# Attention scores with the halves of Q stacked on the contraction axis: two 256-column matmuls for a batch entry instead of three, the low part applied by ScalarE and the mask by GpSimd

## What is computed

```python
x = x + einsum('bct,bcd->bdt', x, w0[idx])          # 32 batch entries of 128 x 1024
q, k, v = heads(x @ Wq.T), heads(x @ Wk.T), heads(x @ Wv.T)   # 16 heads of 64
scores = einsum('bhqd,bhkd->bhqk', q * min(cond, 4), k) / sqrt(64)
attn = softmax(where(causal, scores, lowest))         # 128 x 128 per head
x = x + merge(einsum('bhqk,bhkd->bhqd', attn, v)) @ Wo.T
```

## Time and profile before

| what | value |
|---|---|
| median of 3 runs | 1558.01 us (1557.51 to 1558.75) |
| the profiled execution | 1558.96 us |
| its span, first to last instruction | 1557.5 us |
| PE busy | 1547.1 us (99%), 7459 matmuls |
| DVE, ACT, POOL busy | 1034.9, 840.9, 866.6 us (66, 54, 56%) |
| mean granted clock | 0.998 |

### The profile page before, as it was taken

One profiled execution on the slowest core, in us unless ns is written; L12 is line 12 of the kernel. 1 busy time (PEld: TensorE's weight loads), 2 busy tenths in 40 slices (PEclk: granted clock), 3 DMA queues, 4 the chain that ended last, 5 costly groups with the idle time before them and its releaser, 6 DMA issues.

```text
span 1557.5 us, 23477 instructions
## 1 busy us (share of the span) xinstructions
PE 1547.1 (99%) x7459; PEld 1302.0 (84%) x7459; DVE 1034.9 (66%) x1891; ACT 840.9 (54%) x2286; POOL 866.6 (56%) x752
## 2 busy tenths in 40 slices
PE   9999999999999999999999999999999989999999
PEld 7888888888888888888888888888888878888887
DVE  5867677664477777777767777777777644555553
ACT  6666566652466666666655666666666622222220
POOL 1555665662365566557655576575577545555552
PEclk9999999999999999999999999999999999999999
DMA  9968988866766677767677466677665696444442
GB/s 324 335 230 278 319 307 296 294 254 231 273 190 198 201 214 209 205 184 191 182 240 229 147 179 202 194 200 200 180 188 157 237 366 226 162 168 163 162 167 83
DMA packets 192300, 341.46 MB, mean 219 GB/s; under 512 B 23986, under 2 KB 116402, under 8 KB 185010
## 3 DMA queue, kind: packets, MB, share of 16 engines
q1 hardware_dynamic: 191026, 331.59, 66.2%
q10 hardware_dynamic: 1152, 8.39, 1.4%
HBM read 184.70 MB, written 134.22 MB: 205 GB/s over the span
## 4 chain that ended last, share of the span: by engine, by line
PE 95%; DVE 2%; DMA 1%; SPq 1%; POOL 0%; issue 0%; ACT 0%; DVEq 0%; POOLq 0%
PE p_PJ L768 22%; PE p_PJ L769 22%; PE p_PJ L770 22%; PE p_SC L770 6%; PE p_SC L769 6%; PE p_SC L768 6%; PE p_PV L873 4%; PE p_LP L768 1%; PE p_PV L768 1%; PE p_PV L770 1%; PE p_PV L769 1%; PE p_LP L770 1%; PE p_LP L769 1%; DVE t_WSL L1285 1%; DVE t_TS L1281 1%; DMA out<-t_xr 0%
## 5 line engine op out<-in xcount | busy, mean ns | idle before, releaser
L769 PE MATMUL p_PJ<-t_XL,t_WH 128*128 128x512 f32 x1008 | 394.2, 391 | 0.0
L768 PE MATMUL p_PJ<-t_XH,t_WH 128*128 128x512 f32 x1008 | 394.2, 391 | 0.0
L770 PE MATMUL p_PJ<-t_XH,t_WL 128*128 128x512 f32 x1008 | 392.1, 389 | 0.0
L1118 ACT ACTIVATE t_PP<-t_PP,t_st 128x128 f32<-128x128 f32 x512 | 199.5, 391 | 174.9 <-DVE t_st L1314 173.3
L1438 POOL TENSOR_TENSOR t_PP<-t_PP,t_st 128x512 f32<-128x512 f32 x128 | 133.2, 1041 | 205.8 <-DVE t_st L1318 205.8
L770 PEld LDWEIGHTS p_PJ<-t_XH,t_WL 128*128 128x128 f32 x1008 | 189.3, 188 | 40.5
L768 PEld LDWEIGHTS p_PJ<-t_XH,t_WH 128*128 128x128 f32 x1008 | 190.0, 188 | 33.8
L769 PEld LDWEIGHTS p_PJ<-t_XL,t_WH 128*128 128x128 f32 x1008 | 190.0, 188 | 32.3
L1332 DVE TENSOR_REDUCE t_AT<-p_PV 64x256 f32<-64x512 f32 x252 | 171.3, 680 | 24.5 <-ACT t_AC L1136 12.1
L1444 POOL TENSOR_TENSOR t_AT<-t_AT,t_AC 128x256 f32<-128x256 f32 x126 | 117.1, 929 | 126.2 <-DVE t_AT L1332 126.2
L1441 POOL TENSOR_TENSOR t_PS<-t_PT,t_PS 128x512 fp32r<-128x512 f32 x122 | 157.6, 1292 | 0.0
(11 more groups left out here) (259 smaller groups left out, 3597.7 us busy)
## 6 DMA issues: line engine op xcount, KB each, us to landing
t_XH<-xth_scratch SPq DMA_DIRECT2D x56, 512.0 KB, 6.4
t_XL<-xtl_scratch SPq DMA_DIRECT2D x56, 512.0 KB, 6.7
t_PT<-t_TB SPq DMA_DIRECT2D x580, 32.0 KB, 2.3
v_scratch<-t_VR SPq DMA_DIRECT2D x64, 256.0 KB, 4.6
xth_scratch<-t_XH SPq DMA_DIRECT2D x16, 1024.0 KB, 4.5
xtl_scratch<-t_XL SPq DMA_DIRECT2D x16, 1024.0 KB, 6.8
t_VX<-v_scratch SPq DMA_DIRECT2D x32, 512.0 KB, 5.6
at_scratch<-t_AT SPq DMA_DIRECT2D x126, 128.0 KB, 3.4
```

The costliest lines, as they stand in the source:

```text
L768: pe.matmul(bank, lh, rh, start=first, stop=False, skip_group_check=goes_on)
L769: pe.matmul(bank, lh, rl, start=False, stop=False, skip_group_check=goes_on)
L770: return pe.matmul(bank, ll, rh, start=False, stop=last, skip_group_check=goes_on)
L1118: act.activation(PP[:, u, h, :], PP[:, u, h, :], ACT.Exp, bias=st[:, 0, u, h:h + 1], scale=1.0, accum_out=st[:, 1, u, h:h + 1]).then_inc(a ...
```

## The change

Q's high half of one head (64 rows) and its low half (64 rows) are stacked on the 128 rows of the contraction axis in `QM[h]`; `KM[h]` holds K's high half twice in its first 128 columns, and in the other 128, on the high rows only, its low half (the rest zeros). One matmul per head with 256 columns then gives (qh*kh + ql*kh) in the first 128 columns and qh*kl in the other. The two parts have to be added afterwards: ACT writes beta times the second part into `PP`, POOL adds the mask, and DVE adds beta times the first part. The scores of one batch entry now fill a bank of their own, three banks in turn, `SC[0]`, `SC[1]`, `LP`.

```diff
-        KH = sb("KH", [128, GB, 256], f32r)
-        KL = sb("KL", [128, GB, 256], f32r)
-        QH = sb("QH", [128, T], f32r)
-        QL = sb("QL", [128, T], f32r)
+        KM = [sb(f"KM{h}", [128, GB, 256], f32r) for h in range(2)]
+        QM = [sb(f"QM{h}", [128, T], f32r) for h in range(2)]
...
-                late = 2.5 if n else 0
+                late = 5 if n else 0
                 q_ev.put(done + late, n)
                 ql_ev.put(done + late + 1, n)
                 done += 8
                 kh_ev.put(done + 0.25, n)
                 kl_ev.put(done + 1, n)
-                a = done + 5
+                a = done + 7
                 for u in range(GB):
-                    k = u // 2
-                    sc_at.put(a + k, GB * n + u)
-                    mask_at.put(a + 1 + 2 * k, GB * n + u)
-                    exp_at.put(a + (2, 3, 4, 5)[u], GB * n + u)
-                move_at.put(a + 10, n)
+                    sc_at.put(a + (0, 0.5, 1, 4.5)[u], GB * n + u)
+                    low_at.put(a + (0.75, 1.25, 1.75, 5.25)[u], GB * n + u)
+                    add_at.put(a + (1.25, 2, 3, 6)[u], GB * n + u)
+                    mask_at.put(a + (2.5, 3.5, 4.5, 7.25)[u], GB * n + u)
+                    exp_at.put(a + (3.5, 4.5, 5.5, 8.25)[u], GB * n + u)
+                move_at.put(a + 12.5, n)
                 for k in range(2):
                     P = 2 * n + k
-                    recip_at.put(a + 4 + 2 * k, P)
-                    norm_at.put(a + 4.25 + 2 * k, P)
-                    turn_at.put(a + 7.5 + 1.5 * k, P)
+                    recip_at.put(a + (6.25, 9.25)[k], P)
+                    norm_at.put(a + (6.5, 9.5)[k], P)
+                    turn_at.put(a + (9, 12)[k], P)
                     last = n == 4 * NGRP - 1
-                    half_at.put(a + (20 if last else 25.25) + 0.5 * k, P)
-                    ptl_at.put(a + (20.75 if last else 26) + 1.5 * k, P)
-                    v = a + (27.25 + 3.25 * k if last else 29 + 4.5 * k)
+                    half_at.put(a + (22.5 if last else 26) + 0.5 * k, P)
+                    ptl_at.put(a + (23.25 if last else 26.5) + 1.5 * k, P)
+                    v = a + (29.25 + 3.25 * k if last else 29 + 4.5 * k)
                     own = v + (1.75 if n >= 4 * NGRP - 2 else (1.75, 8.5)[k])
...
-            early = t - PAIR
+            early = t - PAIR + (5 if q == 0 else 0)
...
+        def s_bank(U):
+            return (SC[0], SC[1], LP)[U % 3][:].rearrange("p (h l k) -> p h l k", h=2, l=2)
...
+                pe.wait_ge(act_k, 4 * n + 4)
...
-            three(SC[z][:, 256 * (u % 2):256 * (u % 2) + 256], QH[:, cols], QL[:, cols], KH[:, u, :], KL[:, u, :], True, True).then_inc(pe_sc, 1)
+            if U >= 3:
+                pe.wait_ge(dve_s, U - 2)
+            for h in range(2):
+                mm = pe.matmul(s_bank(U)[:, h].rearrange("p l k -> p (l k)"), QM[h][:, cols], KM[h][:, u, :], start=True, stop=True)
+            mm.then_inc(pe_sc, 1)
...
                     for h in range(2):
                         r = slice(64 * h, 64 * h + 64)
-                        act.activation(KH[r, :, 128 * h:128 * h + 128], pj[r], ACT.Copy).then_inc(act_k, 1)
+                        other = slice(64 - 64 * h, 128 - 64 * h)
+                        act.activation(KM[h][r, :, 0:128], pj[r], ACT.Copy).then_inc(act_k, 1)
+                        act.activation(KM[h][other, :, 0:128], pj[r], ACT.Copy).then_inc(act_k, 1)
...
-                    act.activation(QH[:], PJ[bank_of["q", n]][:], ACT.Copy).then_inc(act_q, 1)
+                    for h in range(2):
+                        r = slice(64 * h, 64 * h + 64)
+                        act.activation(QM[h][r], PJ[bank_of["q", n]][r, :], ACT.Copy).then_inc(act_q, 1)
+                for U in low_at(tick):
...
+                    act.wait_ge(pe_sc, U + 1)
...
+                    act.activation(PP[:, u], s_bank(U)[:, :, 1], ACT.Copy, scale=beta[:, bb:bb + 1]).then_inc(act_l, 1)
...
                 for n in ql_ev(tick):
-                    dve.wait_ge(act_q, n + 1)
-                    dve.tensor_tensor(QL[:], PJ[bank_of["q", n]][:], QH[:].bitcast(f32), ALU.subtract).then_inc(dve_q, 1)
+                    for h in range(2):
+                        r, other = slice(64 * h, 64 * h + 64), slice(64 - 64 * h, 128 - 64 * h)
+                        dve.wait_ge(act_q, 2 * n + h + 1)
+                        dve.tensor_tensor(QM[h][other], PJ[bank_of["q", n]][r, :], QM[h][r].bitcast(f32), ALU.subtract).then_inc(dve_q, 1)
                 for U in mask_at(tick):
...
-                    dve.scalar_tensor_tensor(
-                        out=PP[:, u], in0=SC[u // 2][:, 256 * (u % 2):256 * (u % 2) + 256].rearrange("p (h k) -> p h k", h=2), scalar=beta[:, bb:bb + 1],
-                        in1=mask[:].unsqueeze(1).to_broadcast([128, 2, 128]), op0=ALU.mult, op1=ALU.add).then_inc(dve_s, 1)
+                    dve.wait_ge(pool_m, U + 1)
+                    dve.scalar_tensor_tensor(out=PP[:, u], in0=s_bank(U)[:, :, 0], scalar=beta[:, bb:bb + 1],
+                                             in1=PP[:, u], op0=ALU.mult, op1=ALU.add).then_inc(dve_s, 1)
...
+                for U in add_at(tick):
...
+                    pool.wait_ge(act_l, U + 1)
+                    pool.tensor_tensor(PP[:, U % GB], PP[:, U % GB], mask[:].unsqueeze(1).to_broadcast([128, 2, 128]), ALU.add).then_inc(pool_m, 1)
```

More of the change, by code:

```diff
@@ L205, in cond_attention @@
         act_Y, pool_Y = sem("y_high"), sem("y_low")
+        act_l, pool_m = sem("s_low"), sem("s_low_masked")
         dve_s, dve_m, act_e, dve_r = sem("masked"), sem("row_max"), sem("exp"), sem("row_recip")
@@ L211, in cond_attention @@
         dve_ix, dve_beta, pool_z = sem("index"), sem("beta"), sem("zeroed")
-        l_ix, l_ident, l_mask, l_cond = sem("load_ix"), sem("load_ident"), sem("load_mask"), sem("load_cond")
+        l_ix, l_ident, l_const = sem("load_ix"), sem("load_ident"), sem("load_mask_and_cond")
         l_x = [sem(f"load_x{n}") for n in range(4)]
@@ L237, in cond_attention @@
         step_at, sc_at, pv_at = At(), At(), At()
-        mask_at, exp_at, recip_at, norm_at, turn_at, move_at, half_at, ptl_at, other_at, own_at, at_at = (At() for _ in range(11))
+        low_at, add_at, mask_at, exp_at, recip_at, norm_at, turn_at, move_at, half_at, ptl_at, other_at, own_at, at_at = (At() for _ in range(13))
         q_ev, ql_ev, kh_ev, kl_ev, v_ev, v_store, v_split = (At() for _ in range(7))
@@ L654, in operand @@
             else:
-                halves = QH[:], QL[:]
+                halves = QM[0][:], QM[1][:]
             return tuple(four(h) for h in halves)
@@ L758, in pe_wait_bank @@
             if kind == "q":
-                pe.wait_ge(dve_q, i + 1)
+                pe.wait_ge(dve_q, 2 * i + 2)
             elif kind == "k":
@@ L857, in pe_scores @@
                 pe.wait_ge(dve_g, 5 * (NP - 2))
-            z = u // 2
-            three(SC[z][:, 256 * (u % 2):256 * (u % 2) + 256], QH[:, cols], QL[:, cols], KH[:, u, :], KL[:, u, :], True, True).then_inc(pe_sc, 1)
+            if U == 2:
+                pe.wait_ge(dve_X, 2 * B)
+            if U >= 3:
[3 more added lines that the diff above has]
+            mm.then_inc(pe_sc, 1)
         def pe_values(U):
@@ L1112, in act_program @@
                             act.wait_ge(s_x1[z], 16 * x1_stores(z))
-                    act.activation(QH[:], PJ[bank_of["q", n]][:], ACT.Copy).then_inc(act_q, 1)
+                    for h in range(2):
+                        r = slice(64 * h, 64 * h + 64)
+                        act.activation(QM[h][r], PJ[bank_of["q", n]][r, :], ACT.Copy).then_inc(act_q, 1)
+                for U in low_at(tick):
+                    n, u = divmod(U, GB)
+                    bb = GROUP[n // NC] * GB + u
+                    act.wait_ge(pe_sc, U + 1)
+                    if U == 0:
+                        act.wait_ge(dve_beta, 1)
+                    if n and u == 0:
+                        act.wait_ge(dve_t, 2 * n)
+                    act.activation(PP[:, u], s_bank(U)[:, :, 1], ACT.Copy, scale=beta[:, bb:bb + 1]).then_inc(act_l, 1)
                 for U in exp_at(tick):
@@ L1234, in dve_program @@
                 if tick == 8 * TICK:
-                    dve.wait_ge(l_cond, 16)
+                    dve.wait_ge(l_const, 32)
                     dve.tensor_scalar(beta[:], beta[:], 4.0, HD ** -0.5, ALU.min, ALU.mult).then_inc(dve_beta, 1)
@@ L1404, in pool_program @@
                         pool.wait_ge(s_x1[z], 16 * x1_stores(z))
-                    pool.memset(KH[:].bitcast(f32), 0.0).then_inc(pool_z, 1)
-                    pool.memset(KL[:].bitcast(f32), 0.0).then_inc(pool_z, 1)
+                    pool.memset(KM[0][:].bitcast(f32), 0.0).then_inc(pool_z, 1)
+                    pool.memset(KM[1][:].bitcast(f32), 0.0).then_inc(pool_z, 1)
                 if tick == (T_ATT - 8) * TICK:
@@ L1432, in pool_program @@
```

(9 more changed lines are left out.)

12 lines of the change are left out of this document (3 added, 9 removed).

## The result

The changed kernel takes 1929.76 us (median of 4 runs, 1928.55 to 1930.6) against 1558.38 us: a ratio of 1.238, 95% interval 1.236 to 1.240. Predicted were 1890 us, between 1690 and 1975. The direction and the place were right; of the cases that the prediction lists, the one that came true is its third rival (1937 us, the clock falls in every cell, chance 0.22), not the one it called likeliest (0.56). The stated range holds both.

What follows compares the result with a forecast made beforehand. PE was taken as the bound, busy 99%, time being the sum of matmul spacings. 1559.0 - 30.2 + 223 + 27 + 19 + 45 + 48 = 1891, less 1.0 for the median: 1890 us, range 1690 to 1975.

Steps and rivals of the forecast that it cites:

- third rival: Attention: the clock falls in each cell, 186 us in place of 45 + 48, POOL delays hidden; 1937 us, chance 0.22.
- the one it called likeliest: Attention: values wait in every cell, clock low in only some; 1890 us, own range 1750 to 1925, chance 0.56.
- What it saves: Scores on PE: one matmul less for each of 256 batch-entry scores, at 0.118 us, 30.2 us saved.
- Late exp 3 and the K copies: ACT's queue: exp 3 ends 2.44 us after the k block, K copies follow; values 3.6 us late, 223 us in 62 cells.
- The waits in sum: PE's waits in attention: 223 us for late values, 27 for V work, 19 for `O_add`.
- Cells with extra POOL work: POOL's queue: two V pieces ahead of the first mask addition cost 1.8 us per group, 27 us; `O_add` adds 19 us.
- the 16 `O_add` cells: POOL's queue: each `O_add` stands between the first and second mask addition and costs 1.2 us, 19 us in all.
- The clock: PE after the waits: a fall costs 3 us; 45 us for 15 long waits, 48 us for 16 others.
- "a third": Of the 47 cells without the longer waits, 16 were taken to lose the clock, 3 us each, 48 us.
- The price of the low part: ACT's copies of 256 columns from PSUM: four per cell, taken as 0.38 us each, upper bound 0.618.

Runs made afterwards that it cites:

- run 7: The kernel before without the score matmul of Q's low half with K's high half, all else unchanged: 1529.85 us.
- Runs 1: The kernel after with DVE's reading of the pair's second old values moved from slot 1 to 12.5, for cells below 56: 1910.7 us.
- run 2: The kernel after with ACT's halves of the probabilities moved to slot 15, ahead of exp 3 and the K copies, POOL's first to 15.5: 1925.8 us.
- run 3: The kernel after with the earlier reading of the old values, for all cells, and the earlier halves of the probabilities together: 1676.68 us.
- run 4: The kernel after with only Q low on DVE moved from slot 14 to 14.5, behind mask 3: 1818.8 us.
- 8: The kernel after without ACT's second copy of K's high half: 1829.0 us.
- Run 6: The kernel after with 16 unused matmuls of 512 columns put into PE's queue before the first values of a cell: 1856.3 us.
- 5: The kernel after with old values read earlier, ACT's halves at slot 15.5, Q low behind mask 3, POOL's first sum behind mask additions: 1648.04 us.
- 9: The kernel after with old values read earlier, Q low behind mask 3, halves at slot 15.5, values later, V work spread in most groups: 1710.08 us.
- 10: The kernel after with old values read earlier, Q low behind mask 3, halves at slot 15.5, values at slots 5 and 10; V work unmoved: 1689.27 us.
- the twelfth: The same run as run 12: 1633.92 us.
- run 11: The kernel before with ACT's halves of the probabilities moved from slot 14.25 to 1, behind the K copies, POOL's to 1.5; nothing added: 1674.6 us.
- run 12: The kernel of run 10 with POOL's sum of the first values and its store at slot 9.25 in place of 8: 1633.92 us.

## Why the prediction was right, and 40 us short, point by point

- **What it saves**: 30.2 us predicted, 28 us measured by itself (run 7).
- **Late exp 3 and the K copies**, the mechanism, was right: counted from the last k matmul's end, exp 3 at 1.66 and measured 1.69, K copies done 4.81 and 5.04, POOL's half 6.77 and 6.90, DVE's reduction 6.91 and 7.21, values 7.0 and 7.35. Exp 3 took 0.91 us in place of 0.78 (1010.36 to 1011.27), the copies 0.62 from start to start in place of 0.60; with the pick-ups this makes the difference. So a plain cell's values are 3.93 us late, not 3.6. Runs 1 to 4 and 8 show each member of the chain: both branches, Q low ahead of mask 3, the second K copies.
- **The waits in sum**: 223 + 27 + 19 = 269 us were predicted. PE's idle time in attention is 258 us, and with the 0.16 us that each record overhangs 268. That the two agree is luck: the 62 waits of 3.93 us alone make 244 where 223 was charged, and about 9 us lie in a few other waits; together they fill the place of the 27 that are missing.
- **Cells with extra POOL work**: the term of 27 us for V work is not there in the kernel after, whose wait is 3.79 us with and without it. Run 6 shows that the delay exists, and that it comes out when the clock holds. It was expected to hide in one cell of two; it hid in all. The waits of the 16 `O_add` cells are 0.8 to 1.0 us longer, where 1.2 was predicted: 15 us for 19.
- **The clock** is the term that was mis-sized. The prediction charged 3 us to 15 long waits and to "a third" of the other 47, 93 us. It fell in all of them. What remains of the 370.5 us is 370.5 + 30.2 - 268 = 133 us, 2.1 us in each of the 62 cells: more cells, less in each. The trace bears this out: PE works 280 us at 1.2 GHz, and half of that is 140. A fall costs less than the 3 us taken from the earlier trace rows because in 26 of the 63 cases the stretch is 3.4 us long and not 6.8. The reason given for the third, that the wait is shorter than the 3.95 us of the earlier trace rows, was no reason: run 4 shows falls behind 2.5 us. The prediction itself set beside it that the clock fell 2.8 us after the last matmul, and took a third all the same. The rule of the Trainium skill that the prediction weighed, in "TensorE: Matmul & The Clock Gate", section "HAM oscillation — how this bites in real kernels", says that every burst behind such a wait starts slow; the trace after agrees with it, in 62 cells of 62.
- **The price of the low part**, taken as 0.38 us, is 0.467, inside the bounds given. It hardly mattered, for ACT's chain before exp 3 had 1.83 us to wait for the maximum anyway.

So the 40 us missing are the clock's, and the rest of the sum is right only because its errors met. The third rival came within 8 us in the same way: it has 223 us of waits and 186 of clock, measured are 268 and 133. That ACT's chain is what holds the cell was right for the kernel after. That the order could be mended cheaply was my expectation in runs 3, 5, 9 and 10, and wrong each time: each wait taken away uncovered another. Whether some other order or another division of the work (K's second copy made by a fourth engine, say) gets the 28 us stays open; the twelfth is only the best of five orders tried.

## What to carry to other kernels

Averages of busy time say little when each engine has one in-order queue and the critical one is always fed just in time: before adding an instruction, list what stands behind it in its queue and how many matmuls later the array wants that. When an instruction's inputs come from the array's own most recent block, everything behind it in that queue inherits the wait, so put work whose inputs are long there ahead of it. Price a wait of TensorE here at its idle time, plus about 0.3 us for the restart (0.29 worked out in run 3, and 0.27 in run 11, where 116 us came from 100 us more of idle time in 62 waits), plus, for waits of some 2 us and more, what the clock takes: 2.1 us each in the kernel after.

## What the runs showed of the hardware

The length of PE's idle time goes far to say whether the clock falls, though not all the way. No fall stood behind the 62 waits of 1.26 to 1.72 us in run 11 or the 29 of 1.3 to 1.6 us in run 6. In run 3 one of 144 waits of up to 1.86 us was followed by one, the longest:

```profile
415.00:417.00 2.00, 2.00 (x7) 1.81 (x8) 0.58 (x2) 0.90 (x2) 0.80 (x2) 0.50 0.05 12
```

Of the 12 waits of 1.85 to 2.22 us in run 4, 6 were followed by a fall, of the 7 of about 2.25 us in run 12, 5, of the 7 of about 2.6 us in run 6, 4; but all 34 of about 2.5 us in run 4 were, all 44 of 2.65 us in run 8, and all 62 of 3.7 to 5.3 us in the kernel after. The longest wait that the clock outlasted is one of 3.41 us in run 4:

```profile
1460.74 0.71 PE L882 MATMUL p_PV<-t_PS,t_VV 128*128 128x256 f32 x4 [3.41 <-DVE t_AT L1350]
```

```profile
1458.00:1460.00 2.00, 0.00 (x0) 0.00 (x0) 1.48 (x3) 2.00 (x4) 1.31 (x2) 1.00 0.00 0
1460.00:1462.00 2.00, 1.26 (x8) 1.16 (x9) 1.30 (x2) 0.90 (x3) 1.61 (x3) 1.00 0.00 0
1462.00:1464.00 2.00, 2.00 (x12) 1.75 (x11) 1.38 (x2) 0.48 (x2) 2.00 (x2) 1.00 0.32 98
```

So from about 1.9 to 3.4 us a wait may or may not take the clock down, and what decides it these runs do not show. The stretch at 1.2 GHz was 3.4 us long behind the waits of 2.5 us in run 4, and 3.4 or 6.8 us behind the waits of 3.8 us in the kernel after. The slow matmuls were perhaps not all loss: the delay of 1.3 to 1.6 us that cells behind V work show in run 6 is not there in the kernel after.
